# Weight splits of the last FFN beside the expert tiles, and a last phase that starts with pooling, gathers and its first group

## The reference

```python
x = x + tanh(g_xattn[0]) * L0_xattn(layernorm(x), ctx, ...)   # 8 heads, softmax attention
x = x + tanh(g_ffn[0])   * L0_ffn(layernorm(x), ...)          # shared FFN + 2 of 8 experts per row
x = x + tanh(g_xattn[1]) * L1_xattn(layernorm(x), ctx, ...)   # gates, below
x = x + tanh(g_ffn[1])   * L1_ffn(layernorm(x), W1, W2, W3)   # below

# L1_xattn: block-diagonal gates, and a softmax pooling of the context over its 64 rows
gate_x, gate_a = sigmoid(block_diag(x, w_input)), sigmoid(block_diag(x, w_a))
log_a = -8 * softplus(a_param) * gate_a;  a = exp(log_a)
return a * pooled(ctx) + x * gate_x * sqrt(1 - exp(2 * log_a))

# L1_ffn: W1, W3 (1024, 256), W2 (256, 1024), all fp32
return fwht(silu(x @ W1.T) * (x @ W3.T)) @ W2.T     # fwht: Walsh-Hadamard over 1024, / sqrt(1024)
```

## Time and profile before

| | us |
|---|---|
| median of 3 runs | 1603.46 (1603.43 to 1603.86) |
| the profiled execution's own time | 1603.07 |
| its span in the trace | 1601.4 |
| PE, share of the span busy | 91% |
| DVE / ACT / POOL | 60% / 49% / 33% |
| SP's queue, MB moved | 75.69 |
| POOL's queue, MB moved | 29.89 |

### The profile page before, as it was taken

How to read it: one execution, slowest core, us unless ns; L and a number is a source line. 1 busy time by engine, 2 the same in 40 slices (tenths; PEclk the granted TensorE clock), 3 DMA queues, 4 the chain that set the end, 5 groups by cost and what they waited for, 6 DMA issues and landing times. The chain is left out here.

```text
span 1601.4 us, 32051 instructions
## 1 busy us (share of the span) xinstructions
PE 1450.3 (91%) x10096; PEld 1207.3 (75%) x10097; DVE 957.3 (60%) x1819; ACT 779.5 (49%) x1427; POOL 525.7 (33%) x586
## 2 busy tenths in 40 slices
PE   4899999999999958999898999999916599999998
PEld 3677777777777737888787888888805478888887
DVE  6888887878888726766664333333323366666643
ACT  3466666666666653332233333333313366666652
POOL 4332332323323113644356333200041355555220
PEclk9999999999999987999999999999955599999999
DMA  5122122121121112211373323211170001111000
GB/s 170 57 58 63 50 62 55 52 61 53 53 62 52 45 33 67 92 54 53 122 235 109 92 92 92 66 52 52 44 244 0 27 27 40 40 41 40 15 14 27
DMA packets 89017, 106.54 MB, mean 67 GB/s; under 512 B 12144, under 2 KB 80368, under 8 KB 88304
## 3 DMA queue, kind: packets, MB, share of 16 engines
q1 hardware_dynamic: 79488, 75.69, 15.8%
q0 software_dynamic: 9456, 29.89, 5.8%
HBM read 54.29 MB, written 25.03 MB: 50 GB/s over the span
## 5 line engine op out<-in xcount | busy, mean ns | idle before, releaser
L422 ACT ACTIVATE e_t<-st_ps 128x512 f32<-128x512 f32 x512 | 277.9, 595 | 165.4 <-PE st_ps L527 164.9
L369 DVE TENSOR_REDUCE row_max<-s_ps 128x4 f32<-128x1024 f32 x256 | 311.0, 1217 | 34.0 <-PE s_ps L510 33.8
L510 PE MATMUL s_ps<-k_st,q_st 96*128 96x256 f32 x1024 | 197.2, 316 | 14.3 <-DMA q_st<-q_part 13.0
L527 PE MATMUL st_ps<-q_st,k_st 104*128 104x256 f32 x1024 | 170.4, 287 | 1.6 <-ACT e_t L422 1.5
L510 PEld LDWEIGHTS s_ps<-k_st,q_st 96*128 96x128 f32 x1024 | 147.9, 194 | 23.2 <-DMA q_st<-q_part 13.7
L527 PEld LDWEIGHTS st_ps<-q_st,k_st 104*128 104x128 f32 x1024 | 143.9, 190 | 6.6 <-ACT e_t L422 5.2
L546 PE MATMUL o_ps<-e_t,v_st 128*32 128x256 f32 x2048 | 137.1, 385 | 0.9 <-ACT e_t L422 0.9
L1576 POOL DMA_INDIRECT gathered_tail<-sorted_results,result_at x64 | 72.9, 1139 | 153.5 <-POOLq L2046 135.2
L1434 PE MATMUL y_ps_moe<-w_all_moe,h_hi_moe 128*128 x568 | 112.5, 281 | 2.6 <-DVE h_lo_moe L1253 2.6
L1810 DVE TENSOR_TENSOR h_all_tail<-silu_tail,u_ps_tail 128x512 f32<-128x512 f32 x64 | 43.8, 685 | 117.4 <-ACT silu_tail L1684 65.9
L1259 DVE TENSOR_TENSOR h_all_moe<-silu_moe,u_ps_moe 128x512 f32<-128x512 f32 x71 | 48.8, 687 | 106.2 <-PE u_ps_moe L1412 106.2
(11 more groups left out here) (309 smaller groups left out, 3583.2 us busy)
## 6 DMA issues: line engine op xcount, KB each, us to landing
k_st<-k_part SPq DMA_DIRECT2D x384, 32.0 KB
q_st<-q_part SPq DMA_DIRECT2D x96, 128.0 KB, 3.2
stage_moe<-in_experts POOLq DMA_DIRECT2D x21, 512.0 KB, 4.2
rows_in_moe<-sorted_rows SPq DMA_DIRECT2D x71, 128.0 KB, 2.0
sorted_results<-y_sb_moe SPq DMA_DIRECT2D x71, 128.0 KB
c_in<-in_ctx SPq DMA_DIRECT2D x33, 128.0 KB, 2.1
xn_moe<-in_ctx SPq DMA_DIRECT2D x8, 512.0 KB
context_tail<-in_ctx SPq DMA_DIRECT2D x4, 1024.0 KB, 15.3
```

What stands on the lines that cost most here:

```text
L369: nc.vector.tensor_reduce(out, s_ps[s_ // 2 % 2][:].rearrange("p (j h) t -> p j h t", j=2), AX_X, ALU.max).then_inc(s["max_taken"], 1)
L422: nc.scalar.activation(e_t[h % 8][:], st_ps[h % 2][:], ACT.Exp, scale=float(DH) ** -0.5)\
L510: last = nc.tensor.matmul(s_ps[s_ // 2 % 2][:, 2 * (h - s_) + half_, :], q_st[r][0:ROWS, u, half_ * P:(half_ + 1) * P], k_st[r][0:ROWS, u, ...
L527: last = nc.tensor.matmul(st_ps[h % 2][:, half_, :], k_st[r][0:MROWS, u, j, half_ * P:(half_ + 1) * P], q_st[r][0:MROWS, u, :], start=True ...
```

## The change

Nothing of the computation is changed; instructions are moved, and tiles with them.

- **W1 and W3** are split by GpSimd during the expert tiles: after `rotate`, it issues their two loads (`bring_last`; the second waits for the store of the half-rotated W2, whose tile it reuses) and splits one half after expert 4's pieces and one after expert 5's (`split_last`). The split weights lie where the shared FFN's `xt_hi1/2`, `xt_lo1/2`, `h_hi` and `h_lo` lay; the expert tiles' hi and lo of h move into `xt_hi0` and `xt_lo0`.
- **SP** in the last phase loads the small parameters, the context in eight DMAs of 512 KB, and the half-rotated W2 last, into a tile of its own, without a wait.
- **TensorE** starts with five of eight parts of the pooling; the other three stay behind the gates of group 0. The four rotation rounds go into step -1, after m = 1, 3, 5 and 6. ScalarE's and DVE's parts of them go into step -1 too: ScalarE's behind `decays(0)` (m = 1), ahead of the norm of group 1 (m = 3), at m = 5, and ahead of the FFN norm of group 0 (m = 6); DVE's behind `use_gate(0)` (m = 2), ahead of the shift of group 1 and `make_y(0)` (m = 3), ahead of `update(0)` (m = 5) and ahead of the shift of the FFN norm (m = 6).
- **DVE** starts with softplus and the gate weights' split, then group 0.

```diff
@@ experts(), GpSimd
+            def bring_last(p):
+                if p == 1:
+                    pool.wait_ge(w2_stored, 16)
+                else:
+                    pool.wait_ge(r2["butterflies"], 6)
+                pool.dma_start(w13_raw[p], dram["w13"][p]).then_inc(w13_in[p], 16)
+
+            def split_last(p):
+                pool.wait_ge(w13_in[p], 16)
+                pool.wait_ge(s["down_done"], CHUNKS * GROUPS)
+                nc.gpsimd.tensor_copy(w13_hi[:, p, :], w13_raw[p]).then_inc(r2["w13_high"], 1)
+                pool.wait_ge(r2["w13_high"], p + 1)
+                nc.gpsimd.tensor_tensor(w13_lo[:, p, :], w13_raw[p], w13_hi[:, p, :].bitcast(F32), ALU.subtract)\
+                    .then_inc(r2["w13_low"], 1)
...
                 if k == 3:
                     rotate()
-            pool.wait_ge(w2_stored, 16)
+                    bring_last(0)
+                    bring_last(1)
+                if k in (4, 5):
+                    split_last(k - 4)
+            pool.wait_ge(r2["w13_low"], 2)
@@ gate_and_ffn(), SP
-            sp.dma_start(stage[0][:], dram["w13"][0]).then_inc(piece_in[0], 16)
...
-            sp.dma_start(stage[1][:], dram["w13"][1]).then_inc(piece_in[1], 16)
-            for r in range(4):
-                sp.dma_start(context[:, 8 * r:8 * r + 8, :], rows[:, 8 * r:8 * r + 8, :])\
+            per = TILES // PARTS
+            for r in range(PARTS):
+                sp.dma_start(context[:, per * r:per * r + per, :], rows[:, per * r:per * r + per, :])\
                     .then_inc(context_in[r], 16)
-            sp.wait_ge(s["piece_split"], 1)
-            sp.dma_start(stage[0][:], half_rotated).then_inc(piece_in[2], 16)
+            sp.dma_start(w2_half[:], half_rotated).then_inc(w2_in, 16)
@@ ScalarE
-            for p in range(2):
-                act.wait_ge(piece_in[p], 16)
-                nc.scalar.copy(w_hi[:, p, :], stage[p][:]).then_inc(s["piece_high"], 1)
-            for n in range(4):
+            def take_rotated(n):
                 act.wait_ge(s["rotated"], n + 1)
...
                     if m == 0 and is_group(st + 1):
                         decays(st + 1)
+                    if st == -1 and m in (1, 3):
+                        take_rotated(m // 2)
                     if m == 2 and is_group(st + 1):
                         root(st + 1)
...
+                    if st == -1 and m in (5, 6):
+                        take_rotated(m - 3)
                     if m == 6 and is_group(st + 1):
                         norm_of("ffn", st + 1)
@@ DVE
-            for p in range(2):
-                dve.wait_ge(s["piece_high"], p + 1)
-                nc.vector.tensor_tensor(w_lo[:, p, :], stage[p][:], w_hi[:, p, :].bitcast(F32), ALU.subtract)\
-                    .then_inc(s["piece_split"], 1)
-            for n in range(4):
+            def rotated_low(n):
                 dve.wait_ge(s["rotated_high"], n + 1)
...
+                            select_pooled()
                         use_gate(st + 1)
+                    if st == -1 and m in (2, 3):
+                        rotated_low(m - 2)
+                    if st == -1 and m in (5, 6):
+                        rotated_low(m - 3)
                     if m == 3 and is_group(st + 2):
                         shift_of("gate", st + 2)
@@ TensorE
-            rotate()
+            add_up(range(0, 5))
+            pe.wait_ge(small_in, 64)
             pe.wait_ge(s["gate_split"], 1)
             for st in STEPS:
                 if st == 0:
-                    pe.wait_ge(s["piece_split"], 2)
+                    pe.wait_ge(s["rotated_low"], 4)
...
+                    if st == -1 and m in (1, 3):
+                        rotate(m // 2)
                     if m == 4 and is_group(st + 2):
                         turn("gate", st + 2)
                     if m == 5 and is_group(st + 1):
                         turn_back(st + 1)
+                    if st == -1 and m in (5, 6):
+                        rotate(m - 3)
...
                 if st == -2:
-                    add_up()
+                    add_up(range(5, PARTS))
```

More of the change, by code:

```diff
@@ L686, in experts @@
         w2_in, w2_stored = sem("w2_in"), sem("w2_stored")
+        w13_in = [sem(f"w13_in{r}") for r in range(2)]
         s = {name: sem(name) for name in
@@ L696, in experts @@
               "turned hi_taken lo_taken gate_done up_done silu_done product_done h_turned h_high h_low "
[L697 removed]
+              "down_done y_taken butterflies w13_high w13_low".split()}
         pooling = {name: sem("pool_" + name) for name in
@@ L1463, in sem @@
             return nc.alloc_semaphore(name + "_tail")
-        w_hi = sb("w_hi", [P, 3, PIECE], F32R)
-        w_lo = sb("w_lo", [P, 3, PIECE], F32R)
-        stage = [sb(f"stage{r}", [P, PIECE]) for r in range(2)]
+        w13_hi, w13_lo = w13
+        w2_hi = sb("w2_hi", [P, PIECE], F32R)
+        w2_lo = sb("w2_lo", [P, PIECE], F32R)
+        w2_half = sb("w2_half", [P, PIECE])
         hadamard = sb("hadamard", [P, P])
@@ L1979, in down, with rotate, add_up @@
                 last.then_inc(s["down_done"], 1)
-            def rotate():
-                pe.wait_ge(small_in, 64)
-                pe.wait_ge(piece_in[2], 16)
-                for n in range(4):
-                    wait_count(pe, s["rotated_low"], n)
-                    nc.tensor.matmul(rotated_ps, hadamard[:], stage[0][:, n * GROUP:(n + 1) * GROUP],
-                                     start=True, stop=True).then_inc(s["rotated"], 1)
-            def add_up():
-                for n in range(TILES):
-                    if n % 8 == 0:
-                        pe.wait_ge(context_in[n // 8], 16)
+            def rotate(n):
+                if n == 0:
+                    pe.wait_ge(w2_in, 16)
+                wait_count(pe, s["rotated_low"], n)
+                nc.tensor.matmul(rotated_ps, hadamard[:], w2_half[:, n * GROUP:(n + 1) * GROUP],
+                                 start=True, stop=True).then_inc(s["rotated"], 1)
+            def add_up(parts):
+                per = TILES // PARTS
+                for n in range(parts[0] * per, parts[-1] * per + per):
+                    if n % per == 0:
+                        pe.wait_ge(context_in[n // per], 16)
                     for half_ in range(2):
@@ L2045, in program, with sb @@
             attention(nc, dram, x, ident, tanh_gain)
+        with ExitStack() as early:
+            def sb(name, shape):
+                return early.enter_context(nc.sbuf_tensor(name + "_moe", shape, F32R))
+            flow = ([sb(f"xt_hi{r}", [P, 2, GROUP]) for r in (1, 2)], [sb(f"xt_lo{r}", [P, 2, GROUP]) for r in (1, 2)],
+                    sb("h_hi", [P, FF // P, GROUP]), sb("h_lo", [P, FF // P, GROUP]))
+        w13 = [ctx.enter_context(nc.sbuf_tensor(f"w13_{part}", [P, 2, 2 * FF2], F32R)) for part in ("hi", "lo")]
         with nc.cleanup_on_exit():
-            experts(nc, dram, x, ident, tanh_gain, xs, ys, result_at, shares, attn, half_rotated)
-        gate_and_ffn(nc, dram, x, ident, tanh_gain, ys, result_at, shares, attn, half_rotated, out)
+            experts(nc, dram, x, ident, tanh_gain, xs, ys, result_at, shares, attn, half_rotated, flow, w13)
+        gate_and_ffn(nc, dram, x, ident, tanh_gain, ys, result_at, shares, attn, half_rotated, w13, out)
 def layouts(a):
```

53 lines of the change are left out of this document (28 added, 25 removed).

## The result

| | before | after |
|---|---|---|
| median, us | 1603.45 | 1566.74 |
| runs, lowest to highest | 1603.1 to 1603.86 | 1564.62 to 1569.35 |
| the profiled execution's own time | 1603.07 | 1564.62 |
| its span | 1601.4 | 1562.6 |

The account below looks back on a forecast made before the run. The prediction took the 117 us ramp of waits before the last FFN's first product to set the end, TensorE bounding elsewhere. 1603.46 less 40.1 us (26.1 + 18.4 - 4.4) gave 1563.4 us, range 1555 to 1574, about 85%.

Parts of the forecast that it names:

- Part 1: Expert tiles: splitting W1 and W3 there costs 0; splits 6.9 us a half, store wait 4 to 17 us, both hidden.
- Rival (c): Expert tiles: the splits don't hide, both halves' 13.8 us fall on the tiles, 1577 us; chance 5%.
- Part 2: Front of last phase: group 0's variance step moves from 1212.22 to 1186.1 us, -26.1 us; bounds 1184 and 1189.
- The 1.4 us: Gathers beside DVE's eight combines: by the port lock rule they could cost 3.25 us, making the sum 1.4 us worse, 1564.8.
- The cost of 0 for the front pooling: TensorE, ahead of group 0's transposes: 80 pooling instructions take 16.6 us, end at 1185.6, cover 4.4 us; upper bound 6 us.
- Part 3: Pooling behind group 0's gates: 48 instructions instead of 128, 6.2 us instead of 24.6, -18.4 us.
- Rival (a): Moved pooling: low clock for all 48 instructions, +3.7 us, or late context, up to +6: 1567 to 1570 us; chance 20%.
- rival (b): Front pooling keeps the clock high from group 0's transposes on; the 48 take 4.6 us, -5.0 us, 1558.4; chance 10%.
- Part 4: End of pooling to first FFN product: rotation rounds now inside, 28.0 us become 32.4, +4.4 us; bounds 0 and 10.
- T: The end of pooling, forecast at 1204.1 us, from which the rotation rounds and the steps up to the first FFN product are counted.
- Sum: Whole kernel: 26.1 + 18.4 - 4.4 = 40.1 us gained, 1563.4 us; chance as summed 55%.
- Rival (d): FFN groups: rotations chop TensorE's work, low clock holds through the first groups; 1602.5 or, from the second on, 1641 us; chance 4%.

Follow-up runs that it names:

- e2: Changed kernel with both W1 and W3 loads issued behind expert 4's pieces and each split one expert later; 1571.63 us, 0.9773 of the kernel before.
- e6: Changed kernel's new order alone, with W1 and W3 still loaded and split in the last phase as before; 1574.40 us, 0.9783 of the kernel before.
- e1: The changed kernel again without an edit, on another chip; 1572.85 us, 0.9781 of the kernel before.
- e9: e8 with GpSimd's eight gathers of group 2 put behind its variance step of group 0's FFN norm; 1564.45 us, 0.9708 of the kernel before.
- e5: W1 and W3 splits moved beside the expert tiles, last phase in the old order, W2 loaded ahead of the context; 1594.79 us, 0.9890 of the kernel before.
- e3: Changed kernel with only the second load and its wait for the store put behind expert 4's pieces; 1569.85 us, 0.9763 of the kernel before.
- e4: Changed kernel with both loads behind expert 4's pieces, the wait for the store left ahead of expert 4's splits; 1577.04 us, 0.9799 of the kernel before.
- e10: e9 with W2's load issued only behind group 0's norm; 1571.05 us, 0.9743 of the kernel before.
- e11: e9 with four instead of five of eight pooling parts in front; 1566.70 us, 0.9744 of the kernel before.
- e8: e2 with the rotation rounds also put behind the chain's steps on DVE, ScalarE and TensorE; 1568.43 us, 0.9743 of the kernel before.

## Why the prediction came out as it did

**The bound.** Right. Nearly all of the change's effect but these 4.2 us of the expert tiles lies between the first gather and the first product; behind it the groups take 323.8 us, as before (324.7).

**Part 1, cost 0: the step that failed.** The splits were hidden, as said: 1.91 and 4.59 us for a half, 6.5 against 6.9 forecast, and e2 with both of them has 305.0 us. The wait was seen too, 4.29 us inside the forecast 4 to 17. What failed is "I charge nothing for contention, upper bound 2 us". I compared DVE's busy time in stretches with and without splitting, an average over many tiles. The tiles' own DVE steps (`xt_lo`, `h_lo`, `h_all`) each read one operand from a tile that TensorE has written (`t_ps`, `u_ps`), and those that ran wholly inside a copy or a subtract of GpSimd, 22 after the change, took the same 0.42 and 0.69 us as the others; so that average could not show what the eight steps suffer, which run once. And I asked of the wait only whether the weights behind it would be late. They were not. It costs by when they are split, and that measured 3.1 to 3.9 us of the 4.2.

That DVE holds until GpSimd's instruction ends is what the two timelines show (873.76 and 873.71). The Trainium skill, "SBUF — State Buffer", section "Who interferes with whom", says it so: a two-input DVE instruction needs the read port that GpSimd uses, whoever issued first keeps it for the whole instruction, and the other fully blocks. The trace agrees in who waits and for how long. It does not show the order of issue so plainly: the step at 869.84 starts 0.27 us ahead of the copy and still ends behind it. I had weighed this page for the gathers alone, not for the splits. Rival (c), 13.8 us from splits that don't hide, named the right place and the wrong mechanism.

**Part 2, -26.1.** Measured -28.2, which is the better one of the two bounds that I gave (1184 us): no gather took 1.9 us any more (0.95 to 1.10, all sixteen), though DVE's combines run among them. The 1.4 us that I worked out from the lock rule did not come, but that was my working and not the rule. The traces show a gather held only for what is left of the two-input DVE instruction inside which it starts. Before, the gather at 1175.70 ended 0.83 us behind a subtract of W's split that ended at 1176.76, and e6, which keeps this split on DVE, has its 1.89 and 1.90 us again. A combine lasts 0.48 us and three of the sixteen gathers started in one, so they lost 0.3 us in all. After the change the same is seen in one of the later gathers, beside `make_y` (DVE's timeline, then GpSimd's):

```profile
1213.87 1.22 DVE L1816 SCALAR_TENSOR_TENSOR rest_tail<-gated_tail,rest_tail 128x1024 f32<-128x1024 f32 x1
```

```profile
1214.44 1.47 POOL L1599 DMA_INDIRECT gathered_tail<-sorted_results,result_at  x1 [0.30 <-issue]
```

The DVE step is over at 1215.09 and the gather at 1215.91. The same section offers, as an inference, that descriptor generation needs the write interface and a two-input DVE instruction takes the read interface. The gathers beside W's split wait all the same. They also read their indices from a tile, and no run here tells which of the two waited.

The cost of 0 for the front pooling held with nothing to spare. The 80 instructions took 17.2 us (16.6 forecast) and began 7.3 us behind the first gather (5.4 forecast), since the first eighth took 5.74 us to land. They ended at 1191.9, when xn was ready (1191.5). On the other chips this was 1 to 3 us over (e1's 6.5 us behind the variance step).

**Part 3, -18.4.** Measured -17.0: gates 12.3 us instead of 11.8, the 48 instructions 7.1 instead of 6.2. The clock did what it had done before, high up to some 3 us into them (1.00 from 1200 to 1202 us, 0.50 from 1204 us on). The 6.2 was a miscount: I added instruction counts of neighbouring windows, which count one that crosses an edge twice. TensorE's timeline of the kernel before has the first 51 in one row:

```profile
1223.85 8.34 PE L1996 MATMUL y_ps_tail<-attn,context_tail 128*128 128x8 f32 x51
```

Less three at 12/58 us that is 7.7 for 48, and 7.1 came. Rival (a)'s 9.9 and rival (b)'s 4.6 were both wrong. How long the clock stays high there is not the kernel's alone: in e1, the same kernel, it stood at 1.00 over the last 5 us of pooling, and the 48 took 5.4 us.

**Part 4, +4.4.** Measured +3.6, and by the steps named: round 1 and 2 from the end of pooling, turn_back at T + 12.3 (forecast 12.7), round 3 between it and the update, the gathers' 2.8 us given back. e9 shows that the whole term was avoidable: 25.8 us, less than the 28.1 before.

**Sum.** The profiled executions differ by 38.5 us; the forecast was 40.1, so the terms' errors (+4.2, -2.1, +1.4, -0.8, -0.6, -0.9) largely cancel. Without their signs they come to 10 us; that the total is as close as it is, is in part luck. Between the profiled executions' 38.5 and the medians' 36.7, the 1.7 us (unrounded) are the median's distance from the profiled run, 2.1 after the change and 0.4 before: the changed kernel spreads over 4.7 us where the one before had 0.8. Rival (d) did not occur: the clock stood at 1.00 over the 45 us behind the first product, before the change at 0.96.

## What to carry to other kernels

Before a wait goes into the queue of an engine that works ahead, look at what the delayed work will run beside, not only at whether it is still in time: four microseconds with a whole expert's slack behind them cost four microseconds, since a subtract on GpSimd slid under a chain of small two-input DVE steps. A contention that is invisible in busy shares can be large at one place, so search the timeline for the short instructions whose duration varies (0.19 to 1.49 us) and see what ends when they end. And when a chain is shortened, redo its last wait after each step: here the gathers, the rounds and the gathers again were last in turn.

## What the runs showed of the hardware that I had not expected

- **A one-input DVE step can be held too.** In e5 a TENSOR_SCALAR on 128x64 took 2.38 us, against 0.20 in e3, beside a GpSimd subtract that began 0.01 us ahead of it; in e4 one on 128x256 took 2.50 us, against 0.28 in e3. The two TENSOR_REDUCE steps above were not held. DVE's line of e5, then GpSimd's:

```profile
878.96 2.38 DVE L1176 TENSOR_SCALAR result_at<-both_moe 128x64 uint32<-128x64 f32 x1
```

```profile
878.95 2.34 POOL L811 TENSOR_TENSOR w_all_moe<-stage_moe,w_all_moe 128x1024 fp32r<-128x1024 f32 x1
```

- **TensorE stops without a visible reason.** In front of the ramp it did so in e1 for 0.5 to 1.5 us at three places, 3.2 us in all, beside 360 GB/s, and for 1.8 to 3.5 us in the other kernels with pooling in front but e6; it did not in the profiled execution of the kernel after. Full DMA engines are neither enough (e6: 348 GB/s, no stop) nor needed: in the kernel before it stands from 873.58 to 874.75 us beside 6 GB/s. No run here shows what it waits for.
- **The clock of the first group differs, and not by the kernel alone.** Over the 45 us behind the first product it was 0.92 in e9 and e10, 1.00 in e11 and 0.96 in e1 to e8; but the kernel after, which is the kernel of e1, had 1.00 on the first chip. A level of 0.92 there goes with a longer stretch behind the product (327.1 and 330.0 us) and 1.00 with a shorter one (323.8, 323.3). e9 and e11 differ only in one part of pooling; why their clocks differ was not found. Nor was why e10 took 4.3 us more than e8 behind the product.
